# Dropping the product of the two low parts in the scores of the first query tile of an attention kernel

## What is computed

```
x = x + attn(layernorm(x));  x = x + ffn(layernorm(x))
scores = einsum('bqhgd,bkhd->bhgqk', q, k) * scale
bias   = where(rel >= 0, -slopes * sqrt(rel), -inf)      # causal
attn   = softmax(scores + bias);  out = attn @ v;  return out @ w_o
```

## Time and profile before

| | |
|---|---|
| median of 3 runs | 1367.9 us |
| span of the profiled execution, first to last instruction | 1366.6 us |
| outside that span, against the median | 1.3 us |
| TensorE matmuls (PE) busy | 1351.2 us, 99% |
| TensorE weight loads (PEld) busy | 1144.3 us, 84% |
| VectorE (DVE) | 888.9 us, 65% |
| ScalarE (ACT) | 588.0 us, 43% |
| GpSimd (POOL) | 180.0 us, 13% |

### The profile page before, as it was taken

How to read it: one execution, slowest core, us unless ns; L and a number is a source line. 1 busy time by engine, 2 the same in 40 slices (tenths; PEclk the granted TensorE clock), 3 DMA queues, 4 the chain that set the end, 5 groups by cost and what they waited for, 6 DMA issues and landing times.

```text
span 1366.6 us, 22702 instructions
## 1 busy us (share of the span) xinstructions
PE 1351.2 (99%) x7050; PEld 1144.3 (84%) x7050; DVE 888.9 (65%) x2800; ACT 588.0 (43%) x1674; POOL 180.0 (13%) x171
## 2 busy tenths in 40 slices
PE   8999999999999999999999999999999999999997
PEld 7788888888888888888888888888888888888886
DVE  7876666566666556666655566666556666676697
ACT  3655343444434434444344444444444444453443
POOL 5000302003200302003010122003020031002102
PEclk9999999999999999999999999999999999999999
DMA  6100101001100101001010011001010010000003
GB/s 194 35 0 0 40 0 39 0 0 38 38 0 0 31 8 38 0 0 38 1 38 0 1 38 38 0 0 38 0 38 0 0 38 29 28 1 0 1 1 123
DMA packets 23591, 31.23 MB, mean 23 GB/s; under 512 B 2320, under 2 KB 10512, under 8 KB 23568
## 3 DMA queue, kind: packets, MB, share of 16 engines
q1 hardware_dynamic: 23568, 30.94, 7.5%
HBM read 26.74 MB, written 4.19 MB: 23 GB/s over the span
## 4 chain that ended last, share of the span: by engine, by line
PE 93%; DVE 4%; POOL 1%; ACT 1%; issue 1%; DMA 0%; SPq 0%; DVEq 0%; POOLq 0%
PE ps L973 80%; PE ps L1017 6%; PE ps L1053 2%; PE ps L1052 2%; PE ps L1137 1%; PE ps L994 1%; POOL selected L450 1%; DVE prob L703 0%; DVE prob L653 0%; PE ps L1066 0%; ACT dist L502 0%; DVE selected L751 0%; DMA acc<-in_L_attn_hidden_states 0%; DVE dist L737 0%; POOL selected L447 0%
## 5 line engine op out<-in xcount | busy, mean ns | idle before, releaser
L973 PE MATMUL ps<-xnT,wqkv_hi 128*128 (+1 forms) x1568 | 490.6, 394 | 0.0
L973 PEld LDWEIGHTS ps<-xnT,wqkv_hi 128*128 128x128 f32 x1568 | 290.3, 188 | 60.3 <-issue 0.4
L973 PE MATMUL ps<-xnT,wqkv_lo 128*128 (+1 forms) x784 | 307.7, 393 | 0.0
L491 ACT ACTIVATE prob<-prob,negmax 128x128 f32<-128x128 f32 (+1 forms) x512 | 228.1, 449 | 181.2 <-DVE negmax L703 180.6
L973 PE MATMUL ps<-wo_hi,oT_hi 128*128 128x512 f32 x512 | 203.3, 397 | 0.0
L973 PE MATMUL ps<-wo_lo,oT_hi 128*128 128x512 f32 x512 | 200.3, 391 | 0.0
L973 PE MATMUL ps<-wo_hi,oT_lo 128*128 128x512 f32 x512 | 199.6, 390 | 0.0
L668 DVE SCALAR_TENSOR_TENSOR qT_lo<-ps,qT_hi 128x512 fp32r<-128x512 f32 x128 | 88.4, 691 | 153.1 <-ACT qT_hi L475 152.7
L674 DVE TENSOR_TENSOR pT_lo<-ps,pT_hi 128x512 fp32r<-128x512 f32 x192 | 131.3, 684 | 76.3 <-ACT pT_hi L480 76.3
L475 ACT ACTIVATE qT_hi<-ps 128x512 fp32r<-128x512 f32 x128 | 76.6, 599 | 232.8 <-PE ps L973 232.8
L973 PEld LDWEIGHTS ps<-xnT,wqkv_lo 128*128 128x128 f32 x784 | 147.4, 188 | 33.3
(11 more groups left out here) (115 smaller groups left out, 1863.3 us busy)
## 6 DMA issues: line engine op xcount, KB each, us to landing
raw<-in_L_attn_w_o SPq DMA_DIRECT2D x32, 256.0 KB, 2.6
raw<-in_L_attn_w_qkv SPq DMA_DIRECT2D x30, 256.0 KB, 2.6
raw<-in_L_attn_w_qkv SPq DMA_DIRECT2D x60, 64.0 KB, 2.4
acc<-in_L_attn_hidden_states SPq DMA_DIRECT2D x3, 1024.0 KB, 7.9
out<-acc SPq DMA_DIRECT2D x3, 1024.0 KB, 4.4
acc<-in_L_attn_hidden_states SPq DMA_DIRECT2D x4, 256.0 KB, 3.8
w_raw<-in_L_ffn_weight SPq DMA_DIRECT2D x1, 1024.0 KB, 5.5
acc<-in_L_attn_w_qkv SPq DMA_DIRECT2D x2, 256.0 KB, 3.2
```

What stands on the lines that cost most here:

```text
L491: ins = act.activation(s, s, ACT.Exp, bias=negmax[:, n:n + 1], scale=-1.0, accum_out=rowsum[:, n:n + 1])
L973: ins = pe.matmul(dst, l, r, start=start and m == 0, stop=stop and m == n - 1)
```

## The change

In the scores of the first query tile, the second of a head's two matmuls takes only the 128 columns of k_hi as its moving operand, and adds to the left 128 columns of the head's place alone. The product q_lo·k_lo is no longer computed, as it never was for the second query tile. The number of instructions stays the same on each engine, and nothing is moved.

```diff
                     if qt == 0:
                         both = kT[:, 2 * b, :, :]
                         pe.matmul(dst, q_hi, both, start=True, stop=False)
-                        ins = pe.matmul(dst, q_lo, both, start=False, stop=True)
+                        ins = pe.matmul(dst[:, 0:P], q_lo, kT[:, 2 * b, 0, :], start=False, stop=True)
                     else:
```

## The result

The changed kernel takes 1364.09 us (median of 11 runs, 1363.49 to 1364.7) where the kernel before takes 1367.83 us beside it (11 runs, 1365.03 to 1368.7). The ratio is 0.9976, 95% interval 0.9967 to 0.9984: faster by 3.7 us, and a ratio of 1 lies outside the interval. Forecast were 1364.3 us and 3.6 us.

What follows compares the result with a forecast made beforehand. TensorE was taken to bound the kernel from unit 1 to 29; 1.7 plus 1.9 us make 3.6 us off the 1366.6 us span, 1363.0, plus 1.3 for the median: 1364.3 us. Range 1354.5 to 1369.0 us.

Steps and rivals of the forecast that it cites:

- the 209 steps: Shortened q_lo steps followed by a slow weight load: each falls from 0.120 to 0.111 us, 1.9 us in all.
- the sum: Forecast gain over 240 shortened q_lo steps: 1.7 us before quick loads plus 1.9 us before slow loads, 3.6 us.
- rival 2: Full halving: three weight loads could overlap, all 240 steps fall to 0.066 us; 13.0 us gain, 1354.9 us; chance 0.08.
- the piece of eight steps: Sign in the chain: eight score steps that took 0.96 us would take 0.88 us.
- The cover on VectorE: VectorE frees the banks of scores 0 and 1 about 1 us early, so shorter scores run into no wait.
- the 31 steps: Last q_lo step of score 1, before the v transposes' quick load: 0.120 to 0.066 us each, 1.7 us in all.
- Rival 1: The weight load already sets the 0.120 us step; only steps before transposes gain, or none: 1366.2 to 1367.9 us; chance 0.31.
- Rival 3: F32R matmuls under 256 columns run as plain F32, 0.222 us a step: 24.5 us more, 1392.4 us; chance 0.20.
- Units 30 and 31: Chain leaves TensorE for cluster selection on VectorE and GpSimd; savings at scores 4 and 5 there are waited away.

## Why the prediction was right

- **What bounds the kernel.** Right in the main. The chain lies on TensorE from unit 1 to unit 29, the waits are the same, and 3.43 of 3.7 us show up between the scores of unit 1 and unit 30. The 29 units were to give 29 × (0.054 + 7 × 0.009) = 3.4 us. Too simple was that every nanosecond saved between two matmuls comes off the end: with seven short steps, 0.02 us a unit were saved at scores 0 and 1 and given back by the next matmuls, with no wait between.
- **The price of the 209 steps, 0.111 for 0.120 us.** Right in mechanism: behind a short matmul the next load goes off 0.11 us after the one before, as at the F32 matmuls of L1073 from which the price was taken, and with 64 columns as with 128. The size fits where the steps stand among others: the four of the second half save 0.04 us, 0.010 each, against the 0.009 of the sum, and the three of scores 0 and 1 bring 0.03 us (8.24 for 8.27 us) when the fourth is short as well. Without it they bring nothing, and seven steps a unit gave 0.84 us over 29 units where the sum has 1.8. That the whole was met to 0.05 us is therefore in part luck: had the change made those seven alone, the same prices would have promised twice what came.
- **Where it would show.** Wrong. The prediction looked for starts of matmuls 0.111 us behind the q_lo step, but in the timeline the q_hi matmul starts 0.06 us behind it, which by itself looks like rival 2; the wait is in its duration (0.34 us) and, in the chain, in the next step (0.17 us). The 0.11 us stand between the starts of the loads. The estimate of 0.88 us for the piece of eight steps was met: 625.90 to 626.77 is 0.87 us.
- **The cover on VectorE.** It held. One reading is off without consequence: VectorE's last instruction on the bank of score 0 starts at 630.96 us and ends at 631.04.
- **The price of the 31 steps, 0.066 us.** Right: with that step alone the distance fell by 1.54 us for 29 × 0.054 = 1.57, and the first distance of a unit from 8.32 to 8.27 us.
- **Rival 1, no gain worth the name.** Wrong, but near: its 31 steps were real and gave nearly half, and the others brought the remaining 1.9 of the 3.43 us (3.43 - 1.54), though without the 31 they gave only 0.84. The excess of 0.013 us over the columns belongs to the matmul: the interleaved short steps, with the load out of the way, take 0.06 us, and 256-column steps take 0.12 us with a quick load behind them as well.
- **Rival 2, the full halving.** Wrong. That each load lasts 0.19 us and two overlap does not mean a third could be under way: the distance between starts of slow loads never fell under 0.11 us in the stretch shown, with matmuls of 128 columns or of 64. The 107 ns that the Trainium skill gives for a load ("TensorE: Matmul & The Clock Gate", "LDWEIGHTS (loading the stationary operand)") agree with these 0.11 us. The 81 ns that the same page of the Trainium skill gives for a step of load and matmul ("Back-to-back issue gap") were seen in neither place: a short F32R step costs 0.11 us in front of a slow load and 0.06 us in front of a quick one.
- **Rival 3, a slower mode for fewer than 256 columns.** Wrong. L1034 still has 256 records and 256 loads, the duration of the matmul fell with its columns, and no such mode shows at 192, 128 or 64 columns (253, 223 and 193 ns).
- **Units 30 and 31.** The chain still leaves TensorE behind L1054 (L1073 before), to come back at 1242.20 (1246.20 in the earlier trace rows):

```profile
1226.82 0.85 PE ps L1054 x8
...
1242.20 7.80 PE ps L954 x36
```

From L1054's end to there it is 14.53 us, before 14.54 (1246.20 - 1231.66). So this stretch is set by the other engines and passes nothing on. That scores 4 and 5 of these units bring nothing was not tried alone.

What stays open: why the three short steps of scores 0 and 1 gain nothing when the fourth is long. The 0.02 us are gone within the first eleven of the 512-column matmuls behind the block, which take 2.51 us in the changed kernel, 2.52 before and 2.55 there, while the 25 behind them take 4.41 us in all three. What makes those eleven longer or shorter no run tells. One regularity stands in the records. With starts and ends taken to the nanosecond, the common first distance is 8.320 us before, 8.267 with the last step alone, 8.260 with 192 columns, 8.253 with 64 and 8.240 in the changed kernel, and all these differences are whole multiples of 6.67 ns. So what a version saves in a unit arrives in portions. That alone doesn't explain the zero, since 3 × 0.009 us would be four portions.

## What to carry to other kernels

In this kernel, where every matmul loads its own weights, a step costs about the larger of two things: its columns (0.12 us for 256, 0.06 us for 128), and the load for the matmul behind it (0.11 us for a slow one, about 0.06 us for a quick one). Halving the columns of a step that is already nearly as short as the load brings almost nothing; look in the trace for a load with the same duration in front of a short matmul, and read the distance between the starts of the loads there. A saving of hundredths in one place should be followed to the end of the loop's body, since it can be gone a few matmuls later. Short steps pay when something with a quick load stands behind them, such as a transpose, so once matmuls are shortened their order is worth a second look.

## What was not expected

- A short step's wait for weights is shown in the chain on the next instruction: an unchanged matmul of 256 columns went from 0.12 to 0.17 us (0.20 us behind 64 columns).
- Fewer columns than 128 made the kernel no faster: 1148.94 us against 1148.18 us on the long distance.
- A transpose that stands between a short matmul and a slow load takes 0.13 us; between a 256-column matmul and a slow load it takes 0.11 us. In both, the load behind it has just this distance to the next.
- A saving can vanish without a wait: 0.02 us saved at scores 0 and 1 were given back within the next eleven matmuls.
- The common distances between two places in the chain repeat to 0.01 us from one execution to another, while the times of one kernel spread over 3.7 us (1365.03 to 1368.7).
